# A new order of work in layer 0's rounds, with three PSUM banks for projections and one for turned probabilities

## What is computed

```python
h = layer_norm(x, scale, offset)
q, k, v = h @ wq + bq, ctx @ wk + bk, ctx @ wv + bv      # 16 heads of 128
k, v = concat(k, bias_k), concat(v, bias_v)              # one more key: 257
w = softmax(q @ k.T / sqrt(128))                         # per head and sequence
x = x + (w @ v) @ wo + bo
```

## Time and profile before

| what | us |
|---|---|
| median of three runs | 1309.03 |
| lowest and highest run | 1307.08, 1309.49 |
| the profiled execution's own time | 1308.19 |
| span of the profile | 1306.5 |
| TensorE busy in the span | 1167.3 (89%) |
| DVE, ACT, POOL busy | 850.1, 638.9, 656.2 |

### The profile page before, as it was taken

The page is one execution under the profiler, slowest core; times in us unless marked ns, Lnnn a source line. Parts: engine busy times, 40 slices in busy tenths (PEclk is TensorE's granted clock), DMA queues, the critical chain, the costliest instruction groups (busy, mean ns, idle before and its releaser), DMA issues. The chain is left out here.

```text
span 1306.5 us, 20609 instructions
## 1 busy us (share of the span) xinstructions
PE 1167.3 (89%) x7388; PEld 903.0 (69%) x7388; DVE 850.1 (65%) x2097; ACT 638.9 (49%) x1428; POOL 656.2 (50%) x677
## 2 busy tenths in 40 slices
PE   5999999999999999999989859976758998899994
PEld 4788888888888878888778724433436775666664
DVE  5776676766757666667656364995545666676756
ACT  3655555555655555455652114203223673477770
POOL 3655665666646565466762023670012661277760
PEclk9999999999999999999999979998788999899997
DMA  6110221112210121012202000000030000000000
GB/s 205 64 51 17 65 65 49 32 51 65 66 49 19 64 65 49 26 57 65 65 18 80 1 16 1 0 1 1 0 90 1 2 2 2 1 1 2 2 2 33
DMA packets 35110, 47.05 MB, mean 36 GB/s; under 512 B 3865, under 2 KB 22082, under 8 KB 35010
## 3 DMA queue, kind: packets, MB, share of 16 engines
q1 hardware_dynamic: 34640, 44.83, 10.7%
q10 hardware_dynamic: 370, 0.91, 0.2%
HBM read 44.69 MB, written 1.05 MB: 35 GB/s over the span
## 5 line engine op out<-in xcount | busy, mean ns | idle before, releaser
L444 POOL TENSOR_TENSOR a_prob<-a_prob,a_inv_total 128x512 f32<-128x512 f32 x128 | 144.3, 1128 | 216.2 <-DVE a_inv_total L732 216.2
L1583 POOL TENSOR_TENSOR l_scores<-l_scores,l_neg_max 128x512 f32<-128x512 f32 x144 | 147.9, 1042 | 99.4 <-DVE l_neg_max L1573 99.2
L1573 DVE CUSTOM_DVE_ANT_0 l_scores<-psum,mask 128x256 f32<-128x256 f32 x384 | 139.8, 421 | 69.6 <-PE psum L1526 69.6
L637 ACT ACTIVATE a_prob<-psum,a_neg_max 128x257 f32<-128x257 f32 x256 | 119.2, 472 | 92.8 <-DVE a_neg_max L729 91.9
L1604 ACT ACTIVATE l_prob_T<-psum 128x512 f32<-128x512 f32 x192 | 108.8, 590 | 34.3 <-PE psum L1540 34.2
L1540 PE MATMUL psum<-ident,l_scores 128*128 128x128 f32 x768 | 116.4, 290 | 7.0 <-POOL l_scores L1583 3.9
L1540 PEld LDWEIGHTS psum<-ident,l_scores 128*128 128x128 f32 x768 | 85.1, 145 | 41.1 <-issue 18.8
L736 DVE TENSOR_TENSOR a_probT_lo<-psum,a_probT_hi 128x512 fp32r<-128x512 f32 x128 | 87.9, 686 | 23.1 <-ACT a_probT_hi L641 22.6
L729 DVE TENSOR_REDUCE a_neg_max<-psum 128x2 f32<-128x514 f32 x128 | 87.2, 681 | 1.3 <-PE psum L486 1.3
L566 PE MATMUL psum<-ident,a_prob 128*128 128x128 f32 x512 | 77.6, 274 | 6.9 <-POOL a_prob_bias L447 6.9
L641 ACT ACTIVATE a_probT_hi<-psum 128x512 fp32r<-128x512 f32 x128 | 76.7, 600 | 9.3 <-PE psum L566 9.3
(11 more groups left out here) (331 smaller groups left out, 3296.6 us busy)
## 6 DMA issues: line engine op xcount, KB each, us to landing
wk_raw<-in_L_xattn_wk SPq DMA_DIRECT2D x16, 512.0 KB, 6.4
wq_raw<-in_L_xattn_wq SPq DMA_DIRECT2D x16, 512.0 KB, 5.7
wv_raw<-in_L_xattn_wv SPq DMA_DIRECT2D x16, 512.0 KB, 3.8
wo_raw<-in_L_xattn_wo SPq DMA_DIRECT2D x16, 512.0 KB, 4.0
ctx_rows<-in_ctx SPq DMA_DIRECT2D x3, 512.0 KB, 4.3
x_rows<-in_x SPq DMA_DIRECT2D x2, 512.0 KB, 9.5
mask<-in_mask_Bx1xSxS_ff SPq DMA_DIRECT2D x1, 1024.0 KB, 7.9
out_dram<-fin_y SPq DMA_DIRECT2D x4, 256.0 KB, 2.1
```

Source lines behind the costliest of these rows:

```text
L444: pool.tensor_tensor(prob[:, m % 4, :, 0:S], prob[:, m % 4, :, 0:S], rtot[:, m % 4, :].unsqueeze(2).to_broadcast([P, 2, S]), ALU.mult)
L637: act.activation(prob[:, m % 4, q, 0:S + 1], s_bank(g)[:, q, 0:S + 1], ACT.Exp, bias=negm[:, m % 4, q:q + 1], accum_out=tot[:, m % 4, q:q ...
L1573: e = dve.tensor_tensor_reduce(sc[:, i % SC, q, :], s_bank(i)[:, q * S:(q + 1) * S], masks[:, b * NM + q % NM, :], 1.0, BIG, ALU.add, ALU. ...
L1583: pool.tensor_tensor(sc[:, i % SC, :, :], sc[:, i % SC, :, :], m[:, i % SC, :].unsqueeze(2).to_broadcast([P, 2, S]), ALU.subtract).then_in ...
```

## The change

The order of rounds 0 to 14 is rewritten, the helper that spreads the layer norm over the rounds is made finer and moved, and the banks are dealt differently.

```diff
-    base = ("S0 S1 O0 S2 O1 V0 T0 V1 S3 V2 T1 S4 V3 Q0 T2 S5 Q1 K0 T3 S6 K1 A0 T4 A1 "
-            "S7 T5 Q2 Q3 T6 K2 T7 K3 A2 A3").split()
+    base = ("S0 S1 O0 S2 O1 V0 T0 V1 S3 V2 T1 S4 V3 Q0 T2 S5 Q1 K0 T3 S6 K1 S7 A0 "
+            "T4 A1 T5 Q2 T6 Q3 T7 K2 A2 A3 K3").split()
...
-    out = {-1: "C0 C1 X0 X1 K0 Y0 Y1 K1 L0 L1 K2 K3 Q0 Q1 Q2 Q3".split()}
+    out = {-1: "C0 C1 X0 X1 X2 X3 K0 Y0 Y1 Y2 Y3 K1 L0 L1 K2 K3 Q0 Q1 Q2 Q3".split()}
...
-        if i % NQ == 1:
-            order = put(order, 'V1', 'X0')
-            order = put(order, 'V3', 'X1')
-            order = put(order, 'T3', 'Y0')
-            order = put(order, 'T4', 'Y1')
+        if i % NQ < 2:
+            for t in range(HT):
+                order = put(order, f'T{t + 1}', 'XY'[i % NQ] + str(t))
         if i % NQ == 2:
-            order = put(order, 'V1', 'L0')
-            order = put(order, 'V2', 'L1')
+            order = put(order, 'S0', 'L0')
+            order = put(order, 'S2', 'L1')
...
-    NACC = 2
-    acc = lambda n: ps[:, n % 2, :]
+    NACC = 3
+    acc = lambda n: ps[:, (0, 1, 6)[n % 3], :]
...
-    T_BUFS = 2
-    t_bank = lambda g: ps[:, 6 + g % 2, :].rearrange("p (k n) -> p k n", k=4)
+    T_BUFS = 1
+    t_bank = lambda g: ps[:, 7, :].rearrange("p (k n) -> p k n", k=4)
...
-                    if i % NQ == 1:
-                        rstd_of(event_of(i))
                     norm(4)
...
                     norm(7)
+                    if i % NQ == 0:
+                        rstd_of(event_of(i))
...
                             if m == 0:
                                 pe.wait_ge(vec_ok, 2)
-                                pe.wait_ge(acc_free, USE[i - 1, 'K3'] + 1)
-                                pe.wait_ge(acc_free, USE[i - 1, 'Q3'] + 1)
                                 pe.wait_ge(kcols, i + 1)
+                            if b == 0:
+                                pe.wait_ge(acc_free, max(USE[i - 1, f'Q{h}'], USE[i - 1, f'K{h}']) + 1)
...
-                                if m == QUAD - 1:
+                                if m == 2:
                                     key_columns(i + 1)
```

More of the change, by code:

```diff
@@ L249, in layer0_orders @@
             order = put(order, 'V3', 'B0')
-        if i % NQ == 1:
-            order = put(order, 'V1', 'X0')
-            order = put(order, 'V3', 'X1')
-            order = put(order, 'T3', 'Y0')
-            order = put(order, 'T4', 'Y1')
+        if i % NQ < 2:
+            for t in range(HT):
+                order = put(order, f'T{t + 1}', 'XY'[i % NQ] + str(t))
         if i % NQ == 2:
-            order = put(order, 'V1', 'L0')
-            order = put(order, 'V2', 'L1')
+            order = put(order, 'S0', 'L0')
+            order = put(order, 'S2', 'L1')
         out[i] = order
-    out[LOOPS] = "O0 O1 X0 X1 Y0 Y1 G0 L0 L1 G1 F0 F1 F2 F3 F4 F5 F6 F7 G2 G3".split()
+    out[LOOPS] = "O0 O1 X0 X1 X2 X3 Y0 Y1 Y2 Y3 G0 L0 L1 G1 F0 F1 F2 F3 F4 F5 F6 F7 G2 G3".split()
     return out
@@ L709, in key_columns, with aggregate @@
                     ins.then_inc(kcols, 1)
+                def aggregate(e, j):
+                    dve.wait_ge(ln_stat, HT * e + j + 1)
+                    dve.bn_aggr(mv[:, j, :], bn[:, j, :]).then_inc(ln_aggr, 1)
                 def query_weights(j):
@@ L743, in _ @@
                                 else:
-                                    dve.wait_ge(acc_free, USE[i if i == LOOPS else i - 1, 'O1'] + 1)
-                            for j in (2 * m, 2 * m + 1):
-                                dve.bn_stats(bn[:, j, :], chip.x[:, t0 + j, :]).then_inc(ln_stat, 1)
-                            for j in (2 * m, 2 * m + 1):
-                                dve.wait_ge(ln_stat, HT * e + j + 1)
-                                dve.bn_aggr(mv[:, j, :], bn[:, j, :]).then_inc(ln_aggr, 1)
-                            if m == 1:
+                                    dve.wait_ge(acc_free, USE[i, 'O1'] + 1)
+                            dve.bn_stats(bn[:, m, :], chip.x[:, t0 + m, :]).then_inc(ln_stat, 1)
+                            if m:
+                                aggregate(e, m - 1)
+                            if m == HT - 1:
+                                aggregate(e, m)
                                 dve.wait_ge(ln_aggr, HT * (e + 1))
@@ L753, in _ @@
                         elif k == 'Y':
-                            dve.wait_ge(ln_rstd, e + 1)
-                            for j in (2 * m, 2 * m + 1):
-                                dve.tensor_scalar(xn[:, j, :], chip.x[:, t0 + j, :], mv[:, j, 0:1], rstd[:, j:j + 1], ALU.subtract, ALU.mult).then_inc(ln_norm, 1)
-                            if i < 0 and m == 1:
+                            if m == 0:
+                                dve.wait_ge(ln_rstd, e + 1)
+                            dve.tensor_scalar(xn[:, m, :], chip.x[:, t0 + m, :], mv[:, m, 0:1], rstd[:, m:m + 1], ALU.subtract, ALU.mult).then_inc(ln_norm, 1)
+                            if i < 0 and m == HT - 1:
                                 query_weights(0)
```

## The result

| | before | after |
|---|---|---|
| median of four runs each, us | 1309.26 | 1327.3 (1325.03 to 1328.2) |
| ratio of the medians, 95% interval | | 1.0146 (1.0127 to 1.0164) |
| the profiled execution's own time | 1308.19 | 1328.2 |
| span of the profile | 1306.5 | 1326.5 |
| mean granted clock over the span | 0.963 | 0.951 |

The forecast was 1313.7, with a range from 1302 to 1322. The direction was right, the size was not: +18 us against +4.7, and the range did not hold the time.

The account below looks back on a forecast made before the run. Layer 0 was taken to go at the pace of PE's queue; -37.1 + 41.9 + 6.4 + 0.8 - 3.3 - 4.0 = +4.7 on the profiled 1308.19 gave 1312.9, and 0.8 for the median 1313.7 us, range 1302 to 1322.

Parts of the forecast that it names:

- The redone round 7: Round 7 worked out in the new order: turns 5, 6, 7 wait 1.99, 0.61, 0.19, together 2.79 us.
- Rival (a): Rounds 0 to 14: waits at turns 6 and 7 are hidden and the variance step is short; about 1298, chance 0.16.
- the lower clock: Rounds 1 to 14: a lower clock because of the 2 us waits was given nothing of its own in the sum.
- layers 2 and 3, at 0: Layers 2 and 3, from their first score matmul to the end: forecast change of 0 us.
- what goes away, 35.8: Rounds 1 to 14: PE's waits removed by three banks and the new order, 21.5 + 14.3 = 35.8 us.
- what comes, 44.7 in rounds 1 to 14: Added waits: 2.79 us a round at turns 5 to 7, 1.6 per statistics round, 0.8 in all at turn 7.
- The normalising: Layer norm step in its new place, 0.4 us a tile: falls into gaps and costs 0.
- The 0.8 at turn 7: Rounds 2, 6, 10, 14: POOL's own work ahead of turn 7 ends 0.2 us after DVE's release, +0.8 in all.
- the variance step: Layer norm step on DVE in rounds 0, 4, 8, 12, taken as 1.13 us long, within a term of +6.4.
- rival (b): The variance step is short, 3.6 us less, and one term some 1 us lower: 1310, no measurable change, chance 0.16.
- the ends: Opening ahead of and in round 0: -3.3 us; last round, up to its output product: -4.0 us.
- Rival (c): Third bank frees nothing in rounds with a layer norm, DVE's queue being late; half of 21.5 us stays: 1324, chance 0.15.

Follow-up runs that it names:

- the run with fillers: Changed kernel plus sixteen more matmuls ahead of turn 5 in rounds 0 to 14, results not needed: 1320.31 us, 1.0097 of the kernel before.

## Why the prediction was right, and where it failed

**Right: what goes and what comes.** The waits for `a_v_lo`, `a_c_lo`, `a_k_lo` and POOL left rounds 1 to 14, and the turn bank's came. The redone round 7 held within 0.16 us. I count from the start of the rest of `K1`, which is 345.23 in the kernel before and 351.11 after:

| behind the rest of `K1` | forecast | after |
|---|---|---|
| exponentials 6 | 1.38 | 1.39 |
| copy of `A0` | 2.30 | 2.30 |
| maximum 7 | 3.78 | 3.69 |
| rest of turn 4 | 4.29 | 4.29 |
| turn 5 | 5.04 | 5.11 |
| turn 6 | 7.48 | 7.53 |
| turn 7 | 9.50 | 9.66 |

The waits at turns 5, 6 and 7 are 2.06, 0.59 and 0.30 (2.95 in all) against 1.99, 0.61 and 0.19. Rival (a), in which the two short ones are hidden, falls with that.

**Failed: the lower clock, "I give it nothing of its own".** This is the step of the prediction that missed most. Its reason was that the clock stayed at 1.00 with waits of up to 1.5. But those rows say nothing of waits of 2.0, and the sum itself had made one in every round. What came was a clock of 1.2 GHz for 30.7 us of rounds 1 to 14, and the run with fillers measures its cost at 7.7 us. With that in the sum the forecast would have been 1321.4, inside the range, if still below the time. A known way to a loss was left without a price because the trace had no row for it.

**Failed: layers 2 and 3, at 0.** The sum took it that unchanged code behind the change takes unchanged time. It took 3.8 more. The profile of before could not have shown which value comes; it could have told that 34.7 us of that stretch ran at the lower clock, so that its length hangs on more than its instructions. In the changed kernel these are 41.9. Half of the 7.2 more is 3.6, nearly the whole loss there. That the change brought this about is not shown, since the kernel before with a few matmuls more has it too.

**Mis-sized: what goes away, 35.8.** Rounds 3 and 11 have no layer norm and differ from round 7 by the bias product alone: 42.3 against 40.2, so it is worth 2.1 and not 1.90. The trace of before had said so too, where round 3 lasts 40.34 and round 7 38.27. That is 1.4 us of work in seven rounds that I had called waits. Rounds 4, 8 and 12 add another 1.0: in the run with fillers round 4 is 45.25 long and round 7 40.24, and without the 1.25 of longer turns the difference is 3.8 and not the 3.4 of the sum. In all, rounds 1 to 14 kept 2.8 us that the sum had removed; this figure is what is left over when the other terms are taken off, and 0.4 of it is not itemised.

**Mis-sized: what comes, 44.7 in rounds 1 to 14** (14 x 2.79, three times 1.6, and 0.8). At the full clock, in the run with fillers, the turns' waits there are 46.5, and the refill of the pipe behind turn 7 adds 0.11 a round: 48.0. The parts moved against each other. The normalising, which "falls into gaps, 0", puts 0.25 to 0.6 on turns 5 and 6 of rounds 1, 5, 9 and 13. The 0.8 at turn 7 in rounds with POOL's own row came to nothing.

So for rounds 1 to 14: 22.7 - 8.9 = 13.8 = 7.7 (clock) + 3.3 (turns) + 2.8 (removal). With the 3.8 of layers 2 and 3, and 2.3 that the opening, round 15 and what stands behind it came out better than forecast, that is the 15.3 between the +4.7 of the sum and the +20.0 of the profiled spans.

**Right: the variance step.** Round 4 of the changed kernel, DVE, POOL and turn 6, answers to the earlier trace rows:

```profile
231.92 1.04 POOL L442 TENSOR_TENSOR a_prob<-a_prob,a_inv_total 128x512 f32<-128x512 f32 x1
231.94 1.05 DVE L753 TENSOR_SCALAR a_ln_var_eps<-a_ln_mean_var 128x4 f32<-128x4 f32 x1
...
234.39 0.41 PE L564 MATMUL psum<-ident,a_prob 128*128 128x128 f32 x2 [1.51 <-DVE a_probT_lo L738]
```

The step on 4 numbers per partition takes 1.05 us and ends with POOL's multiply that began beside it, so it was long again and rival (b) falls. That agrees with what the Trainium skill says in SBUF — State Buffer, section Who interferes with whom, of a lock between DVE and POOL held for a whole instruction. The round's turns waited 1.3 us more than those of round 7 (0.15 at turn 5, 1.1 at turn 6) against a forecast of 1.6.

**Right: the ends.** In PE's timeline `S2` of round 0 (it started at 36.10 in the kernel before) and the first output product behind round 15, which answers to the earlier trace rows:

```profile
32.16 0.36 PE L482 MATMUL psum<-a_k_hi,a_q_hi 128*128 128x258 f32 x1 [1.25 <-ACT a_prob L635]
...
717.04 0.29 PE L482 MATMUL psum<-a_wo_hi,a_c_hi 128*128 128x256 f32 x1
```

`S2` came 3.9 earlier (forecast 3.3). Round 15 up to the output product takes 717.04 - 674.69 = 42.35, 4.2 less (forecast 4.0).

**Rival (c)** gave 1324, the nearest number, by a reason that the runs deny: with the third bank PE waits for no `V`, `A` or `K` in the rounds with a layer norm, neither in the changed kernel nor in the run with the banks alone. A time that fits does not make the reason right.

## What to carry to other kernels

An engine's order is written once but read by every queue: a score step moved ahead on PE put 0.9 us of exponentials and 0.7 of a maximum in front of a bank's release on ACT and DVE; putting it back by one place gave 18.6 us, and the whole old order 32. Where a list moves, redo by hand what stands ahead of each release, in every queue: with ACT and DVE put right, POOL's queue made turn 7 wait. Banks are worth what the order lets them be: the same swap of one bank cost 4.7 us in rounds 1 to 14 under one order and 15.9 under the other, and shortened round 15 in both; it was best dealt by round. And if a sum makes a wait longer than any in the trace, put a price on the clock too, since the trace of before can't clear it.

## What the hardware showed that was not expected

- Waits of 2 us, with busy work between them, were enough for TensorE to drop to 1.2 GHz eight times in 606 us. In the kernels whose longest wait in rounds 1 to 14 was 1.6 or less it never dropped there. Nor did it in the kernel with the new order and the old banks, which waited 2.0 once in each of rounds 4, 8 and 12, and less elsewhere (clock 1.00), so the length of one wait is not all there is to it. The Trainium skill describes such falls and returns in TensorE: Matmul & The Clock Gate, section HAM oscillation — how this bites in real kernels; the traces agree that a wait that comes back in a loop can bring a fall again and again, though here in eight of fourteen rounds and not in each.
- Stretches at the lower clock can cost less than half their length: in rounds 1 to 14, 30.7 us of them cost 7.7. Part of the slower work falls where PE would wait anyhow: turn 6 waited for nothing in round 2 (146.44), and 0.40 us in round 7 (358.64). The Trainium skill, in TensorE: Matmul & The Clock Gate, section Terms, puts the cost at half, which gives an estimate of some 15 us; the runs decide for 7.7. In layers 2 and 3, 7.2 us more at the lower clock go with 3.8 us more time, which is about half.
- 240 useless matmuls, put where PE waits, made the kernel 7 us faster.
- Layers 2 and 3, untouched, take 300.9 or 304.7 us in most of the profiled executions, with 34.7 or 41.9 us at the lower clock. An effect of 4 us in a kernel like this says nothing until the stretch in which it arose is known.
